# Tokens in another order on chip: keys of strides 2 to 8 side by side, the true order restored for the causal attention

## The chip, the core and the metric

The kernel runs on one core of a Trainium2 chip. The time is the device time of one execution, in microseconds. A core has a matrix engine (TensorE, rows PE, with its weight loads listed apart as PEld), a vector engine (DVE), a scalar engine (ACT), GpSimd (POOL) and the sync engine that issues the DMAs (SP). They work through their own lists of instructions and wait for each other by semaphores.

## The reference

The input is 16 sequences `q` of 512 tokens with 256 features, in fp32. Each goes through two layers: a coupling network of three cycles (A), a causal attention with rotary parts (B), the coupling network again (C), a small feature network (D), an attention with strided keys (E) with its own MLP, and the small network again (F). What matters here is that only B looks at the order of the tokens (rotary tables and causal mask), and that head `h` of E uses every `STRIDES[h]`-th key and value:

```python
STRIDES = [1, 1, 2, 2, 2, 2, 4, 4, 4, 4, 8, 8, 8, 8, 16, 16]
for h, stride in enumerate(STRIDES):
    k_s = k[:, h, ::stride, :]
    v_s = v[:, h, ::stride, :]
    scores = jnp.einsum('bqd,bkd->bqk', q[:, h], k_s) * scale
    attn = jax.nn.softmax(scores, axis=-1)
    outs.append(jnp.einsum('bqk,bkd->bqd', attn, v_s))
```

## The kernel before, in words

Everything of a sequence stays on chip from its load to its store. `X` holds the tokens on partitions (four tiles `t` of 128 tokens), `XT` the transposed normalized tokens: features on partitions, 512 tokens along the free dimension, two halves `f` of the features. Three sequences are on chip at a time. The table `TURN` (L30) is an order written out by hand: one pass over it works on three sequences in turn (A, B and C of newer ones, E and F of older ones), and every engine takes its own part of each step from it in this order. One pass is called a block below; there are 16 of them, some 215 us apart, and the 16 sequences overlap in them.

Token `t*128 + p` lies on partition `p` of tile `t` (L120), so in `XT` the tokens stand in their true order, column by column. Keys of stride `s` are then every `s`-th column. This touches four kinds of products of stage E on TensorE:

- `v.E`, the values (`values_part`, L619): the weights that are loaded are columns of `XT`, picked by `tile_of_keys` (L73). For heads of stride 1 to 4 a tile of 128 keys is every 4th column, for stride 8 and 16 every 8th and 16th. `V_PARTS` (L271) lists the pieces of tile 0: heads 0 to 9 with 128 keys, 10 to 13 with 64, 14 and 15 with 32; then tiles 1, 2 and 3. They stand in `TURN` as `part.E.0`, `part.E.1` and `v.E` (tiles 2 and 3).
- `content.E.g`, keys and queries of four heads (`content`, L582): the moving operand of the keys is `XT[:, c, f, 0:T:step]` with the first stride of the group, 1, 2, 4 or 8.
- `max.E.g`, a first product for the row maxima (`maxima`, L636): the second pair of heads in a group reads every second key of `HI`.
- `exp.E.g.r`, the scores that go to the exponential (`exponents`, L665): the loaded weights are columns of `MAT` by `tile_of_keys`; in group 0 (strides 1, 1, 2, 2) every 4th column, in group 1 every 2nd, in group 2 adjacent ones.

A fp32 product is two matmul instructions with a weight load each, so a call of `mm` on fp32 data shows as two rows of PE and two of PEld.

Around them, ACT copies the transposes from PSUM to `XT` (`copied`, L1066; the branch for B is L1076) and the attention's transposed result to `ATT` (`attended`, L1185; B is L1192). SP stores a finished sequence from `X` and loads the next one into the same place (L1366, L1368), after the wait for F's additions.

Of the kernel before, what the change touches and what calls it, by code (L numbers as in the profile page):

```python
# [14 lines left out]
P = 128  # L15
CH = 3
# [53 lines left out]
    return [[(t + u, (u * n[0], u * n[1]), n) for u in range(m)] for t in range(0, T // P, m)]  # L70


def tile_of_keys(columns, step, stride, t):  # L73


    if stride > 4:
        return columns[:, ::stride // step]
    return columns[:, (0, 2, 1, 3)[t] // step::4 // step]


def exp_rounds(s, g, T):
# [33 lines left out]
def build(nc, ins, out):  # L115
# [1 line left out]
    N, T, C = x_in.shape  # L117
    TT, KT = T // P, C // P
    assert T == 512 and C == 256
    x_v = x_in.rearrange("q (t p) d -> q p t d", p=P)  # L120
    o_v = out.rearrange("q (t p) d -> q p t d", p=P)
    _, e_tiles, _ = attention_shapes("E", T)
    E_SLOTS = sum(e_tiles)
    E_SLOT = [sum(min(n, t) for n in e_tiles) for t in range(TT)]
# [5 lines left out]
    with ctx:  # L130
# [109 lines left out]
        def steps_of(*names):  # L240
# [27 lines left out]
                                               for j in (2 * st[3], 2 * st[3] + 1) if j < 7])  # L268
        g_ready = Signal("g_ready", [st[1:3] for st in steps_of("relu") if st[3] == 3])
        dve_step, pool_step = sem("dve_step"), sem("pool_step")  # L270
        V_PARTS = [(0, 10, 4, 0), (10, 14, 8, 0), (14, 16, 16, 0)] + [  # L271
            (E_SLOT[t], E_SLOT[t] + sum(n > t for n in e_tiles), 1, t) for t in range(1, TT)]

        def tiles_of_groups(count):
# [41 lines left out]
        with nc.Block() as block:  # L316
# [73 lines left out]

            @block.sync
            def _(sp):
                sp.dma_start(X[:, 0], x_v[0]).then_inc(x_loaded[0], 16)
                for dst, src in first_loads:
                    sp.dma_start(dst, src, allow_slow_non_contiguous=True).then_inc(loaded_first, 16)

# [51 lines left out]
        with nc.Block() as block:  # L448

            @block.tensor  # L450
            def _(pe):
# [28 lines left out]
                def product(bank, key, pairs, rows=P, cols_=T):  # L480
                    dst = take(bank, *key)
                    for n, (lhsT, rhs) in enumerate(pairs):
                        last = mm(dst[0:rows, 0:cols_], lhsT, rhs, n == 0, n == len(pairs) - 1)
                    last.then_inc(full[bank], 1)

                def turned(b, key, src):
# [95 lines left out]
                def content(s, q, g):  # L582
                    c = q % CH
                    if s == "E":
                        in_xt("E", q)
                    else:
                        read_out(pe, "kvt", q)
                        read_out(pe, "ql", q)
                    if s == "B":
                        product(single_bank(), ("content", s, q, g, "q"), [(w_qdec[:, g, :], QL[:, q % 2, :])])  # L590
                        b = pair_bank()
                        dst = take(b, "content", s, q, g, "k", width=2)
                        for v in range(2):
                            half = slice(64 * v, 64 * v + 64)
                            last = mm(dst[:, v, 0:T // 2], w_kdec[half, g, :], KVT[half, q % 2, :])
                        last.then_inc(full[b], 1)
                        return
                    for w in "kq":
                        step = STRIDES[4 * g] if w == "k" else 1
                        product(single_bank(), ("content", s, q, g, w),  # L600
                                [(w_qk[:, f, "qk".index(w), g, :], XT[:, c, f, 0:T:step]) for f in range(KT)], cols_=T // step)

                def values(s, q):
                    c = q % CH
# [14 lines left out]
                def values_part(q, t):  # L619
                    c = q % CH  # L620
                    if t == 0:
                        in_xt("E", q)
                        dst = take(single_bank(), "v", "E", q, 0)
                    else:
                        dst = ps[:, J["v", "E", q, 0][0], :]
                    for first, end, stride, tile in V_PARTS:
                        if tile != t:
                            continue
                        h = first - E_SLOT[t]
                        for f in range(KT):  # L630
                            keys = tile_of_keys(XT[:, c, f, :], 1, stride, t)
                            last = mm(dst[0:min(P, T // stride), HD * first:HD * end], keys,
                                      w_v[:, f, HD * h:HD * (h + end - first)], f == 0, f == KT - 1)
                    return last

                def maxima(s, q, g, m):  # L636
                    keys, _, _ = attention_shapes(s, T)
                    if m == 0:
                        pe.wait_ge(hi_ready.sem, hi_ready.at(s, q, g, contents_in[s][-1]))
                    parts = parts_of((s, q, g), hi=True)  # L640
                    rounds = max_rounds(s, g, T)[m]
                    banks = [pair_bank(), pair_bank()]
                    dst = [take(banks[pair], "max", s, q, g, m, pair, width=2) for pair in (0, 1)]
                    for t, first, nk in rounds:
                        for a, b in parts:
                            for j in range(4):
                                at, step = first[j // 2], keys[4 * g] // keys[4 * g + j]
                                row = slice(ROWS * j, ROWS * j + ROWS)
                                last = mm(dst[j // 2][:, j % 2, at:at + nk[j // 2]], HI[row, a, t * P:(t + 1) * P],
                                          HI[row, b, 0:nk[j // 2] * step:step], (a, b) == parts[0],  # L650
                                          s == "E" and (a, b) == parts[-1])
                                if s == "E" and j % 2 and (t, (a, b)) == (rounds[-1][0], parts[-1]):
                                    last.then_inc(full[banks[j // 2]], 1)
                    if s == "B":
                        for pair in (0, 1):
                            for t, first, nk in rounds:
                                at = first[pair] + t * P
                                for b in range(4):
                                    for n in range(2):
                                        row = slice(ROWS * (2 * pair + n), ROWS * (2 * pair + n + 1))  # L660
                                        last = mm(dst[pair][ROWS * b:ROWS * b + ROWS, n, at:at + P], ident_b[row, row],
                                                  mask_q[row, b, :], False, True)
                            last.then_inc(full[banks[pair]], 1)

                def exponents(s, q, g, r):  # L665
# [4 lines left out]
                    for pair in (0, 1):  # L670
# [5 lines left out]
                        for kt, q0, at in exp_rounds(s, g, T)[r][1]:  # L676
                            for a, b in parts:
                                for n in range(2):
                                    j = 2 * pair + n
                                    row = slice(ROWS * j, ROWS * j + ROWS)  # L680
                                    if s == "B":
                                        columns = MAT[row, b, kt * P:(kt + 1) * P]
                                    else:
                                        columns = tile_of_keys(MAT[row, b, 0:T // STRIDES[4 * g]], STRIDES[4 * g],
                                                               STRIDES[4 * g + j], kt)
                                    last = mm(dst[0:m, n, at:at + T - q0], columns, MAT[row, a, q0:T],
                                              (a, b) == parts[0], (a, b) == parts[-1])
                        last.then_inc(full[bank], 1)
# [125 lines left out]
            def _(dve):  # L814
# [13 lines left out]
                def statistics(s, q):  # L828
                    c = q % CH
                    if s == "A":  # L830
                        dve.wait_ge(x_loaded[c], 16 * (q // CH + 1))
                    src = (XN if s == "E2" else X)[:, c]
                    for t in range(TT):
                        last = dve.bn_stats(stats[:, c, t, :], src[:, t, :])  # L834
# [230 lines left out]
            def _(act):  # L1065
                def copied(s, q):  # L1066
                    c = q % CH
                    for f in range(KT):
                        src = when_full(act, "xt", s, q, f)
                        if s in "AC":  # L1070
                            last = act.activation(XT[:, c, f, :], src, ACT.Copy, accum_out=means[:, c, f:f + 1])
                        elif s == "E2":
                            last = act.activation(XT[:, c, f, :], src, ACT.Identity, scale=c_gamma[:, f:f + 1],  # L1073
                                                  bias=c_beta[:, f:f + 1])
                        else:
                            last = act.activation(XT[:, c, f, :], src, ACT.Copy)  # L1076
                        freed(last, "xt", s, q, f)
# [107 lines left out]
                def attended(s, q):  # L1185
# [3 lines left out]
                    for f in range(KT):  # L1189
                        src = when_full(act, "att", s, q, f)  # L1190
                        if s == "B":
                            last = act.activation(ATT[:, f, :], src, ACT.Copy)  # L1192
                        else:
                            last = act.activation(ATT[:, f, :], src, ACT.Identity, bias=c_vb[:, f:f + 1])
                        freed(last, "att", s, q, f)
# [156 lines left out]

            @block.sync
            def _(sp):
                sp.dma_start(X[:, 1], x_v[1]).then_inc(x_loaded[1], 16)
                for dst, src in loads:
                    sp.dma_start(dst, src, allow_slow_non_contiguous=True).then_inc(loaded, 16)
                sp.wait_ge(zeroed, 4)
# [2 lines left out]
                for q in range(2, N):  # L1361
                    c = q % CH
                    if q >= CH:
                        for n in range(2):
                            read_out(sp, "mout", "F", q - CH, n)
                        sp.dma_start(o_v[q - CH], X[:, c]).then_inc(x_stored[c], 16)  # L1366
                        sp.wait_ge(x_stored[c], 16 * (q // CH))
                    sp.dma_start(X[:, c], x_v[q]).then_inc(x_loaded[c], 16)  # L1368
                for q in range(N - CH, N):
                    c = q % CH  # L1370
                    for n in range(2):
                        read_out(sp, "mout", "F", q, n)
                    sp.dma_start(o_v[q], X[:, c]).then_inc(x_stored[c], 16)
                for c in range(CH):
                    sp.wait_ge(x_stored[c], 16 * len(range(c, N, CH)))


# [35 lines left out]
```

## Time and profile before

| | |
|---|---|
| time, median of 3 runs | 3690.88 us (3689.16 to 3691.62) |
| span of the profiled execution, its first to its last instruction | 3688.1 us (its time with what lies around the span is not listed apart; the median of the runs stands 2.8 us above the span) |
| busy: PE, PEld, DVE, ACT, POOL | 94%, 54%, 62%, 51%, 26% |
| chain of work that ended last: PE, DVE, ACT | 82%, 12%, 3% |
| mean granted TensorE clock | 0.965 of 2.4 GHz |
| HBM traffic | 6 GB/s over the span |

Busy time is the share of the span in which an engine had an instruction under way; matmuls are pipelined, so their durations overlap, and what one costs is read from where the next begins. The granted clock is 1.00 (2.4 GHz) or 0.50 (1.2 GHz) at any moment, and a mean in between over a stretch.

### The profile page before, as it was taken

The numbers are of one execution on the slowest core, as the hardware profiler recorded it, in microseconds if no ns is written. First come the engines' busy times: TensorE is split into PE (matmuls) and PEld (weight loads), VectorE is DVE, ScalarE is ACT, GpSimd is POOL, SyncE is SP. The second block draws the span as 40 slices with busy tenths as digits, with TensorE's granted clock in tenths as the row PEclk, the third lists the DMA queues.
The fourth block names the chain that finished last, engine by engine and source line by source line (L and its number), as shares of the span: only waits on it lengthen the run. The fifth ranks groups of instructions, "written<-read, shape, count | busy, mean of one in ns | idle before, by whom it ended". The sixth has DMA issues, their size and how long they took to land.

```text
span 3688.1 us, 63212 instructions
## 1 busy us (share of the span) xinstructions
PE 3457.0 (94%) x24928; PEld 2002.6 (54%) x24928; DVE 2271.7 (62%) x4778; ACT 1887.2 (51%) x2919; POOL 955.1 (26%) x1069
## 2 busy tenths in 40 slices
PE   4789999999999999999999999999999999999876
PEld 3355556565555656555555655555565555555443
DVE  3446576666756666675666667566666756676442
ACT  2234655546465564646556464555646555564422
POOL 2213132331313232131222323122231313223111
PEclk8798999999999999999999999999999999999977
DMA  3000000000000000000000000000000000000000
GB/s 92 1 1 1 1 1 12 1 13 1 13 1 1 13 1 13 1 13 1 1 12 1 13 1 8 5 1 13 1 13 1 1 13 1 12 1 7 1 6 6
DMA packets 40882, 27.73 MB, mean 8 GB/s; under 512 B 19600, under 2 KB 39696, under 8 KB 40592
## 3 DMA queue, kind: packets, MB, share of 16 engines
q1 hardware_dynamic: 40592, 23.69, 2.2%
q8 instruction: 203, 3.33, 0.4%
q14 instruction: 87, 0.71, 0.1%
HBM read 15.30 MB, written 8.39 MB: 6 GB/s over the span
## 4 chain that ended last, share of the span: by engine, by line
PE 82%; DVE 12%; ACT 3%; issue 2%; POOL 0%; DVEq 0%; ACTq 0%; POOLq 0%
PE ps L478 74%; PE ps L489 8%; DVE MX L915 2%; DVE XN L843 1%; ACT other L1200 1%; DVE MX L909 1%; DVE XN L894 1%; DVE XN L891 1%; DVE XT L854 1%; DVE LT L881 1%; DVE XN L892 1%; DVE XT L853 1%; ACT PR L1174 0%; DVE stats L834 0%; DVE other L851 0%
## 5 line engine op out<-in xcount | busy, mean ns | idle before, releaser
L1174 ACT ACTIVATE PR<-ps 128x1024 f32<-128x1024 f32 (+3 forms) x592 | 524.5, 931 | 341.9 <-PE ps L478 340.6
L478 PE MATMUL ps<-MAT 32*128 32x512 f32 (+5 forms) x4928 | 593.3, 503 | 14.4 <-DVE MX L909 4.4
L915 DVE TENSOR_REDUCE MX<-ps 128x2 f32<-128x1024 f32 (+3 forms) x512 | 391.8, 818 | 203.7 <-PE ps L478 201.4
L1246 POOL TENSOR_TENSOR rstd<-var,neg_half 128x4 f32<-128x4 f32 x144 | 148.7, 1033 | 1311.3 <-DVE var L826 1183.5
L478 PEld LDWEIGHTS ps<-MAT 32*128 32x128 f32 (+2 forms) x4928 | 290.4, 199 | 262.4 <-issue 162.7
L478 PE MATMUL ps<-XT,cn_w 128*128 128x256 f32 x1536 | 367.6, 390 | 13.5 <-DVE XT L853 8.5
L478 PEld LDWEIGHTS ps<-XT,cn_w 128*128 128x128 f32 x1536 | 290.5, 193 | 99.7 <-issue 28.7
L478 PE MATMUL ps<-other,cn_w 128*128 128x512 f32 (+2 forms) x1152 | 321.0, 480 | 16.1 <-ACT other L1082 5.4
L921 DVE SCALAR_TENSOR_TENSOR MAT<-ps,MAT 128x512 f32<-128x512 f32 x128 | 88.5, 691 | 300.9 <-PE ps L489 300.3
L1281 POOL TENSOR_TENSOR MAT<-XN 128x512 f32<-128x512 f32 x128 | 167.3, 1307 | 402.4 <-DVE XN L894 241.8
L1304 POOL TENSOR_SCALAR_AFFINE_SELECT PR<-PR 128x512 f32<-128x512 f32 (+1 forms) x192 | 158.8, 827 | 410.0 <-ACT PR L1174 409.8
L909 DVE TENSOR_REDUCE MX<-ps 128x2 f32<-128x1024 f32 (+6 forms) x256 | 220.0, 902 | 59.6 <-PE ps L478 58.8
L1295 POOL CAST HI<-MAT 128x512 fp32r<-128x512 f32 (+3 forms) x256 | 146.4, 585 | 388.2 <-ACT MAT L1141 248.4
L478 PE MATMUL ps<-XT,w_up 128*128 128x512 f32 x512 | 245.7, 611 | 0.9 <-ACT XT L1073 0.9
L478 PE MATMUL ps<-HI 32*128 32x256 f32 (+4 forms) x3072 | 209.2, 360 | 36.4 <-DVE MX L915 25.4
L1082 ACT ACTIVATE other<-ps,cols 128x512 f32<-128x512 f32 x192 | 121.4, 683 | 228.3 <-PE ps L478 228.3
L478 PE MATMUL ps<-w_down,other 128*128 128x256 f32 x1024 | 227.4, 380 | 0.0
L843 DVE TENSOR_SCALAR XN<-X,mv,rstd 128x256 f32<-128x256 f32 x384 | 183.6, 540 | 67.6 <-POOL rstd L1246 67.0
L1200 ACT ACTIVATE other<-ps,cols 128x512 f32<-128x512 f32 x256 | 179.2, 795 | 71.4 <-PE ps L478 71.4
L478 PEld LDWEIGHTS ps<-HI 32*128 32x128 f32 x3072 | 117.3, 192 | 176.3 <-issue 136.5
L478 PEld LDWEIGHTS ps<-w_down,other 128*128 128x128 f32 x1024 | 193.4, 190 | 33.9 <-issue 7.7
L1183 ACT ACTIVATE AO<-ps 128x512 f32<-128x512 f32 x128 | 77.0, 602 | 255.5 <-PE ps L478 255.3
(158 smaller groups left out, 5718.2 us busy)
## 6 DMA issues: line engine op xcount, KB each, us to landing
X<-in_L_attn_x SPq DMA_DIRECT2D x16, 512.0 KB, 3.9
out<-X SPq DMA_DIRECT2D x16, 512.0 KB, 3.0
w_up<-in_L_attn_W SPq DMA_DIRECT2D x1, 1024.0 KB, 6.8
w_down<-in_L_attn_W SPq DMA_DIRECT2D x1, 1024.0 KB, 8.8
w_krope<-in_L_attn_W_krope SPq DMA_DIRECT2D x1, 512.0 KB, 4.4
w_qk<-in_L_attn_Wqkv SPq DMA_DIRECT2D x4, 128.0 KB, 4.4
cn_w<-in_L_ffn_cn_w SPq DMA_DIRECT2D x1, 256.0 KB, 4.2
w_qrope<-in_L_attn_W_qrope SPq DMA_DIRECT2D x1, 256.0 KB, 3.1
```

What stands on the lines that cost most here:

```text
L478: return pe.matmul(dst, lhsT, rhs, start=start, stop=stop, skip_group_check=True)
L489: last = pe.transpose(dst[:, t * P:(t + 1) * P], src(t), ident[:])
L843: last = dve.tensor_scalar(XN[:, c, t, :], src[:, t, :], mv[:, c, t, 0:1], rstd[:, c, t:t + 1], ALU.subtract, ALU.mult)
L909: last = dve.tensor_reduce(MX[:, t0:t0 + len(parts), at], src[:, :, 0:len(parts) * nk].rearrange("p j (t k) -> p t j k", k=nk), AX_X, ALU.max)
L915: last = dve.tensor_reduce(MX[:, t, at], src[:, :, a:a + nk[pair]], AX_X, ALU.max)
L1082: freed(act.activation(H1[:, area_of[s], m, :], src, ACT.Gelu, bias=c_b1[:, m:m + 1]), "h1", s, q, k, m)
L1174: freed(act.activation(PR[0:m, tile_of((s, q, g, r)), 2 * pair:2 * pair + 2, lo:T], ps[0:m, b:b + 2, 0:T - lo], ACT.Exp, scale=SCALE[s]), ...
L1200: last = act.activation(U[:, area_of[s], j, :], src, ACT.Relu, scale=c_mw1[:, j:j + 1], bias=c_mb1[:, j:j + 1])
L1246: pool.tensor_tensor(rstd[:, c, :], var[:, c, :], neg_half[:], ALU.pow).then_inc(rstd_ready.sem, 1)
L1281: pool.tensor_tensor(dst, a, b, ALU.add).then_inc(rope_sum.sem, 1)
L1295: pool.tensor_copy(HI[:, content_tile((s, q, g), w, hi=True), 0:n], MAT[:, content_tile((s, q, g), w), 0:n]).then_inc(hi_ready.sem, 1)
L1304: pool.affine_select(out=p, in_=p, compare_op=ALU.is_ge, fill=0.0, base=0, pattern=[[0, 4], [0, n], [1, P]], channel_multiplier=-1).then_i ...
```

## The change

The token of tile `t` on partition `64*d + m` is now `8*m + 4*d + t`. Tile 0 holds the tokens whose number is divisible by 4, its first half those divisible by 8; tiles 0 and 2 hold the even ones. Loads and stores of `X` are split in two halves of 64 partitions, each with 4 KB in one piece per partition where there were four pieces of 1 KB. In stage E the keys of strides 1 to 8 are adjacent columns; only stride 16 out of the keys of stride 8 still takes every second column. The keys of `content.E` come from whole tiles in the order 0, 2, 1, 3. The values of tile 0 for heads 10 to 13 go with those of heads 0 to 9 in one product of 128 keys and 224 columns, and the rows from 64 on are not read. For B, ACT's copy to `XT` writes the true order (inner step 8 elements, 32 bytes), and its copy to `ATT` goes back (inner step 128 elements, 512 bytes); both read PSUM in order. A, C, D and F don't depend on the order.

```diff
+def keys_in(columns, first_stride, stride, t=0, n=P):
+    if (first_stride, stride) == (8, 16):
+        return columns[:, 0:2 * n:2]
+    return columns[:, t * P:t * P + n]
+def tokens_of_keys(columns, stride):
+    if stride > 2:
+        return columns[:, 0:512 // stride]
+    tiles = columns.rearrange("p (v u n) -> p u v n", v=2, u=2)
+    return tiles[:, 0] if stride == 2 else tiles
+def first_token(t):
+    return (0, 2, 1, 3)[t]
...
-    x_v = x_in.rearrange("q (t p) d -> q p t d", p=P)
-    o_v = out.rearrange("q (t p) d -> q p t d", p=P)
+    x_v = x_in.rearrange("q (m d t) c -> q d m t c", d=2, t=TT)
+    o_v = out.rearrange("q (m d t) c -> q d m t c", d=2, t=TT)
...
-        V_PARTS = [(0, 10, 4, 0), (10, 14, 8, 0), (14, 16, 16, 0)] + [
+        V_PARTS = [(0, 14, 4, 0), (14, 16, 16, 0)] + [
...
-                sp.dma_start(X[:, 0], x_v[0]).then_inc(x_loaded[0], 16)
+                for d in range(2):
+                    sp.dma_start(X[64 * d:64 * d + 64, 0], x_v[0, d]).then_inc(x_loaded[0], 16)
...
                         step = STRIDES[4 * g] if w == "k" else 1
+                        tokens = [tokens_of_keys(XT[:, c, f, :], step) if w == "k" else XT[:, c, f, :] for f in range(KT)]
                         product(single_bank(), ("content", s, q, g, w),
-                                [(w_qk[:, f, "qk".index(w), g, :], XT[:, c, f, 0:T:step]) for f in range(KT)], cols_=T // step)
+                                [(w_qk[:, f, "qk".index(w), g, :], tokens[f]) for f in range(KT)], cols_=T // step)
...
-                            keys = tile_of_keys(XT[:, c, f, :], 1, stride, t)
-                            last = mm(dst[0:min(P, T // stride), HD * first:HD * end], keys,
+                            m = min(P, T // stride)
+                            keys = keys_in(XT[:, c, f, :], 8 if stride == 16 else 1, stride, first_token(t), m)
+                            last = mm(dst[0:m, HD * first:HD * end], keys,
...
-                                          HI[row, b, 0:nk[j // 2] * step:step], (a, b) == parts[0],
+                                          keys_in(HI[row, b, :], *strides, 0, n), (a, b) == parts[0],
...
-                                        columns = tile_of_keys(MAT[row, b, 0:T // STRIDES[4 * g]], STRIDES[4 * g],
-                                                               STRIDES[4 * g + j], kt)
+                                        columns = keys_in(MAT[row, b, :], STRIDES[4 * g], STRIDES[4 * g + j], kt, m)
...
+                        elif s == "B":
+                            last = act.activation(XT[:, c, f, :].rearrange("p (m d t) -> p t d m", d=2, t=TT),
+                                                  src.rearrange("p (t d m) -> p t d m", d=2, t=TT), ACT.Copy)
...
-                            last = act.activation(ATT[:, f, :], src, ACT.Copy)
+                            last = act.activation(ATT[:, f, :].rearrange("p (t d m) -> p m d t", d=2, t=TT),
+                                                  src.rearrange("p (m d t) -> p m d t", d=2, t=TT), ACT.Copy)
...
-                        sp.dma_start(o_v[q - CH], X[:, c]).then_inc(x_stored[c], 16)
-                        sp.wait_ge(x_stored[c], 16 * (q // CH))
-                    sp.dma_start(X[:, c], x_v[q]).then_inc(x_loaded[c], 16)
+                        for d in range(2):
+                            sp.dma_start(o_v[q - CH, d], X[64 * d:64 * d + 64, c]).then_inc(x_stored[c], 16)
+                        sp.wait_ge(x_stored[c], 32 * (q // CH))
+                    for d in range(2):
+                        sp.dma_start(X[64 * d:64 * d + 64, c], x_v[q, d]).then_inc(x_loaded[c], 16)
```

The order of the steps stays as it is. What changes in the lists is one pair of products per block on TensorE and the DMAs on SP. TensorE around the values of stage E, before (`ps` is PSUM, `w_v` the value weights, `x2` counts the calls):

```order
L478 MATMUL ps<-mask_q,ident_b 32x128 x16
L478 MATMUL ps<-w_v,XT 128x160 x2
L478 MATMUL ps<-w_v,XT 64x64 x2
L478 MATMUL ps<-w_v,XT 32x32 x2
L478 MATMUL ps<-PR,VB 17x384 x4
```

and with the change (L494 is the line that was L478):

```order
L494 MATMUL ps<-mask_q,ident_b 32x128 x16
L494 MATMUL ps<-w_v,XT 128x224 x2
L494 MATMUL ps<-w_v,XT 32x32 x2
L494 MATMUL ps<-PR,VB 17x384 x4
L494 MATMUL ps<-HI 128x128 x8
```

The two products of 64 keys went into those of 128. SP at the stores and loads of two blocks, before:

```order
L1366 DMA out<-X 128x4x256
L1368 DMA X<-in_L_attn_x 128x4x256
L1366 DMA out<-X 128x4x256
L1368 DMA X<-in_L_attn_x 128x4x256
L1366 DMA out<-X 128x4x256
```

and with the change:

```order
L1395 DMA out<-X 64x1024 x2
L1398 DMA X<-in_L_attn_x 64x1024 x2
L1395 DMA out<-X 64x1024 x2
L1398 DMA X<-in_L_attn_x 64x1024 x2
L1395 DMA out<-X 64x1024 x2
```

Each store and each load is now two DMAs of half the partitions.

## Rows read from the trace of the kernel before

**Rows 1.** The page: busy time of each engine, and the chain that ended last.

```profile
PE 3457.0 (94%) x24928; PEld 2002.6 (54%) x24928; DVE 2271.7 (62%) x4778; ACT 1887.2 (51%) x2919; POOL 955.1 (26%) x1069
...
PE 82%; DVE 12%; ACT 3%; issue 2%; POOL 0%; DVEq 0%; ACTq 0%; POOLq 0%
```

**Rows 2.** Timeline, weight loads of one block: start us, busy us, what, count.

```profile
1000.23 1.01 PEld L478 LDWEIGHTS ps<-w_v,XT 128*128 128x128 f32 x4
...
1001.38 0.56 PEld L478 LDWEIGHTS ps<-w_v,XT 128*64 128x64 f32 x4
...
1005.30 1.94 PEld L478 LDWEIGHTS ps<-w_v,XT 128*128 128x128 f32 x8
...
1082.70 1.86 PEld L478 LDWEIGHTS ps<-w_kv,XT 128*128 128x128 f32 x16 [0.24 <-issue]
```

**Rows 3.** Timeline, PE: keys and queries together, named by the keys' columns.

```profile
995.41 2.41 PE L478 MATMUL ps<-XT,w_qk 128*128 128x64 f32 x8
...
1014.01 2.88 PE L478 MATMUL ps<-XT,w_qk 128*128 128x128 f32 x8
...
1027.00 2.85 PE L478 MATMUL ps<-XT,w_qk 128*128 128x256 f32 x8
```

**Rows 4.** Timeline, PE: scores of group 1, then of group 0.

```profile
1074.39 1.15 PE L478 MATMUL ps<-MAT 32*128 32x512 f32 x8
...
1089.82 1.26 PE L478 MATMUL ps<-MAT 32*128 32x512 f32 x8
```

**Rows 5.** Waits: engine, line waited for, us in total, times, longest.

```profile
PE ps L570 <- DVE LT L881: 28.8, 16, 3.7
```

**Rows 6.** Stretches: length, busy (count) of PE, PEld, DVE, ACT, POOL, clock, DMA.

```profile
572.00:580.00 8.00, 7.78 (x118) 6.19 (x120) 4.99 (x11) 0.96 (x5) 3.25 (x4) 1.00 0.41 130
...
1007.00:1013.00 6.00, 6.00 (x50) 3.56 (x54) 3.58 (x12) 1.26 (x5) 1.09 (x2) 0.50 0.01 3
```

**Rows 7.** Timeline of SP: stores and a load of `X`, by issue.

```profile
785.79 0.38 SPq L1366 DMA_DIRECT2D out<-X  x1
788.73 0.37 SPq L1368 DMA_DIRECT2D X<-in_L_attn_x  x1
1000.54 0.38 SPq L1366 DMA_DIRECT2D out<-X  x1
...
1217.77 0.38 SPq L1366 DMA_DIRECT2D out<-X  x1
...
1433.61 0.38 SPq L1366 DMA_DIRECT2D out<-X  x1
```

**Rows 8.** Groups of ACT by form: busy us, mean ns, idle before.

```profile
L1174 ACT ACTIVATE PR<-ps 128x1024 f32<-128x1024 f32 x288 | 282.8, 1022 | 247.6 <-PE ps L478 247.2
...
L1076 ACT ACTIVATE XT<-ps 128x512 f32<-128x512 f32 x128 | 71.6, 600 | 101.4 <-PE ps L489 100.0
```

**Rows 9.** Timeline: both copies of B, and the product behind the second one.

```profile
1048.24 1.07 ACT L1192 ACTIVATE ATT<-ps 128x512 f32<-128x512 f32 x2
...
1051.68 3.72 PE L478 MATMUL ps<-w_o,ATT 128*128 128x256 f32 x16
...
1081.00 1.08 ACT L1076 ACTIVATE XT<-ps 128x512 f32<-128x512 f32 x2
```

**Rows 10.** DMA issues by line: count, KB each, median us to landing.

```profile
X<-in_L_attn_x SPq DMA_DIRECT2D x16, 512.0 KB, 3.9
out<-X SPq DMA_DIRECT2D x16, 512.0 KB, 3.0
...
w_qrope<-in_L_attn_W_qrope SPq DMA_DIRECT2D x1, 256.0 KB, 3.1
```

**Rows 11.** Timeline behind that load: statistics, normalization, transposes of A.

```profile
794.72 1.39 DVE L834 BATCH_NORM_STATS2 stats<-X 128x6 f32<-128x256 f32 x4
...
797.86 1.74 DVE L843 TENSOR_SCALAR XN<-X,mv,rstd 128x256 f32<-128x256 f32 x4 [1.13 <-POOL rstd L1246]
...
802.08 1.09 PE L489 MATMUL ps<-ident,XN 128*128 128x128 f32 x8
```

More of the change, by code:

```diff
@@ L70, in max_rounds @@
     return [[(t + u, (u * n[0], u * n[1]), n) for u in range(m)] for t in range(0, T // P, m)]
[L73 to L78, printed above, removed]
+def keys_in(columns, first_stride, stride, t=0, n=P):
[9 more added lines that the diff above has]
+    return (0, 2, 1, 3)[t]
 def exp_rounds(s, g, T):
@@ L482, in product @@
                     for n, (lhsT, rhs) in enumerate(pairs):
-                        last = mm(dst[0:rows, 0:cols_], lhsT, rhs, n == 0, n == len(pairs) - 1)
+                        to = dst[0:rows, 0:cols_]
+                        if len(rhs.shape) == 3:
+                            to = to.rearrange("p (v n) -> p v n", n=P)
+                        elif len(rhs.shape) == 4:
+                            to = to.rearrange("p (u v n) -> p u v n", u=2, n=P)
+                        last = mm(to, lhsT, rhs, n == 0, n == len(pairs) - 1)
                     last.then_inc(full[bank], 1)
@@ L646, in maxima @@
                             for j in range(4):
-                                at, step = first[j // 2], keys[4 * g] // keys[4 * g + j]
+                                at, n = first[j // 2], nk[j // 2]
                                 row = slice(ROWS * j, ROWS * j + ROWS)
-                                last = mm(dst[j // 2][:, j % 2, at:at + nk[j // 2]], HI[row, a, t * P:(t + 1) * P],
-                                          HI[row, b, 0:nk[j // 2] * step:step], (a, b) == parts[0],
+                                strides = (STRIDES[4 * g], STRIDES[4 * g + j]) if s == "E" else (1, 1)
+                                last = mm(dst[j // 2][:, j % 2, at:at + n], HI[row, a, t * P:(t + 1) * P],
+                                          keys_in(HI[row, b, :], *strides, 0, n), (a, b) == parts[0],
                                           s == "E" and (a, b) == parts[-1])
@@ L830, in statistics @@
                     if s == "A":
-                        dve.wait_ge(x_loaded[c], 16 * (q // CH + 1))
+                        dve.wait_ge(x_loaded[c], 32 * (q // CH + 1))
                     src = (XN if s == "E2" else X)[:, c]
@@ L1354, in _ @@
             def _(sp):
-                sp.dma_start(X[:, 1], x_v[1]).then_inc(x_loaded[1], 16)
+                for d in range(2):
+                    sp.dma_start(X[64 * d:64 * d + 64, 1], x_v[1, d]).then_inc(x_loaded[1], 16)
                 for dst, src in loads:
@@ L1365, in _ @@
                             read_out(sp, "mout", "F", q - CH, n)
-                        sp.dma_start(o_v[q - CH], X[:, c]).then_inc(x_stored[c], 16)
-                        sp.wait_ge(x_stored[c], 16 * (q // CH))
-                    sp.dma_start(X[:, c], x_v[q]).then_inc(x_loaded[c], 16)
+                        for d in range(2):
+                            sp.dma_start(o_v[q - CH, d], X[64 * d:64 * d + 64, c]).then_inc(x_stored[c], 16)
+                        sp.wait_ge(x_stored[c], 32 * (q // CH))
+                    for d in range(2):
+                        sp.dma_start(X[64 * d:64 * d + 64, c], x_v[q, d]).then_inc(x_loaded[c], 16)
                 for q in range(N - CH, N):
@@ L1372, in _ @@
                         read_out(sp, "mout", "F", q, n)
-                    sp.dma_start(o_v[q], X[:, c]).then_inc(x_stored[c], 16)
+                    for d in range(2):
+                        sp.dma_start(o_v[q, d], X[64 * d:64 * d + 64, c]).then_inc(x_stored[c], 16)
                 for c in range(CH):
-                    sp.wait_ge(x_stored[c], 16 * len(range(c, N, CH)))
+                    sp.wait_ge(x_stored[c], 32 * len(range(c, N, CH)))
 NAMES = ["L0_attn_x", "L0_attn_W_kv", "L0_attn_g_kv", "L0_attn_W_kdec", "L0_attn_W_vdec", "L0_attn_W_q",
```

## The prediction

> **What bounds the kernel now.** I read the page first: PE is busy 94% of the span and holds 82% of the chain that ended last, DVE 12%, ACT 3% [rows 1]. So time that TensorE saves is nearly all time that the kernel saves, and work added to ACT or SP counts only where it makes TensorE wait. Then the weight loads in a timeline, because the change alters how weights are read. The loads of the values, every 4th column of XT (16 bytes apart), take 1.94 us for 8, or 0.24 us each; the loads of adjacent columns of the same XT for the latent product take 1.86 us for 16, or 0.12 us each [rows 2]. The moving operand shows the same: keys and queries of a group together take 2.85 us with 256 key columns at stride 2, and 2.88 us, no less, with 128 key columns at stride 4; with 64 at stride 8 it is 2.41 us [rows 3]. The queries are the same four matmuls each time, so the step from 2 to 4 doubles what a column costs. Scores with weights at stride 4 take 1.26 us for 8 matmuls, at stride 2 only 1.15 [rows 4]. Stride 2 costs nothing that these rows show, stride 4 twice the time.
>
> **The change part by part, for one of 16 blocks.**
>
> *Values, tiles 1 to 3.* 12 loads (4 for tile 1, 8 for tiles 2 and 3) go from 0.24 to 0.12 us, and their matmuls of 96 and 32 columns are shorter than a load: 12 x 0.12 = 1.44 us.
>
> *Values, tile 0.* Now four loads of 128 keys take from 1000.23 to 1001.38, 1.15 us, and then four of 64 keys 0.56 us [rows 2]. The four of 64 go. The four of 128 get 224 columns instead of 160 and become bound by the stream: the group at 2.85 us streams 4 x 256 and 4 x 512 columns, 0.93 ns a column [rows 3], so 224 columns are 0.21 us and four are 0.84. Of the 1.15 us, 4 x 0.24 were loads and 0.2 the handover to the next shape, which stays: 0.84 + 0.2 = 1.04. Saved: 0.56 + 0.11 = 0.67 us.
>
> *Keys of group 2.* 128 adjacent columns are as short as a load, and so are 64 at stride 8. The group falls from 2.88 to about 2.41: 0.47, of which I take 0.45. Groups 0, 1 and 3 had no stride that costs: 0.
>
> *Scores of group 0.* Four rounds, each from 1.26 to 1.15: 0.44 us. The first round stands ahead of a product (L570) that waits for DVE's scaling of the latent in every block, 28.8 us over 16 [rows 5]; what is won ahead of it is waited for again. That leaves 0.33. Scores of groups 1 to 3 and the row maxima (second pair at stride 2, beside a first pair with twice its columns): 0.
>
> The sum is 1.44 + 0.67 + 0.45 + 0.33 = 2.89 us, and 16 blocks make 46. I take off 4 us for waits that come up at the edges, where few sequences overlap: **42 us**; bounds 35 (a quarter lost to waits) and 48 (the first round counted too).
>
> *The clock.* After the slow loads the granted clock falls to 1.2 GHz in many blocks: 1.00 over the values of the block at 571, but 0.50 from 1007 to 1013 [rows 6]. Nine of the 16 blocks have such a stretch right behind the values, four of 6.8 us and five of 3.4 us. Its price is read from the store that SP issues at the same place of every block: 214.75 us from 785.79 to 1000.54 without a low stretch, 217.23 us to the next with one of 6.8 us, 215.84 us to the next with one of 3.4 us [rows 7]. That is 2.5 and 1.1 us, and 4 x 2.5 + 5 x 1.1 = 15.5 us in all. The loads ahead of the fall now take half the time and the products behind them come sooner. I expect two thirds of the low stretches to go: **10 us**; bounds 0 and 16.
>
> *ACT's copies of B.* 32 copies to XT and 32 to ATT take 0.60 us each now [rows 8] and get inner steps of 32 and 512 bytes. No row shows ACT writing with a step. The near end is 0.60 us unchanged. The far end is the doubling per column that TensorE shows when it reads at 16 bytes [rows 2]: ACT takes 1.02 us for 1024 columns and 0.60 for 512 [rows 8], so 0.42 us goes with the columns and a copy becomes 1.02. That is the nearest row with such a step, so I take it. The pair to XT then ends at 1081.00 + 1.08 + 0.84 = 1082.92 instead of 1082.08 [rows 9], and the latent's loads, at 1082.70 now [rows 2], start some 0.25 us later: 16 x 0.25 = **4 us** lost. The pair to ATT ends at 1049.31 and its reader starts at 1051.68 [rows 9]; 0.84 us more is covered. Behind it on ACT wait the third layer of A and the exponentials of group 3, which come 0.8 us later; their readers on TensorE have other products ahead of them. If that cover is gone it costs up to 0.8 us a block, 13 in all. What speaks against the change here is the Trainium skill, "Advanced Engine Details and Errata", section SBUF Cachelines: an access that goes to another 16-byte line each time pays, and only two hits on a line absorb it. By that rule both copies are slow and the sum loses the 4 us; without it they stay at 0.60 us and it loses none. No row here shows it for writes.
>
> *SP.* Each store and each load becomes two DMAs. At the start and at the end one more issue of about 0.4 us [rows 7] lies open: **1 us**. In between, a load issued at 788.73 lands 3.9 us later [rows 10], at 792.6; DVE begins its statistics at 794.72 and ends the normalization at 799.60, and TensorE wants it at 802.08 [rows 11]. The slack is 2.1 + 2.5 = 4.6 us, less the 2.6 us by which the values and keys ahead of it get shorter: 2.0 us. Two more issues take 0.8. If the halves overlap, 256 KB lands in 3.1 us [rows 10] and nothing is late: 0. If they run one behind the other, the load takes 6.2 instead of 3.9 and the store 6.2 instead of 3.0, 5.5 more, and 4.3 us show in each of 13 blocks, 56 us. I take 0, because 512 KB in one piece lands in 3.9 us, and the bytes are the same. The Trainium skill, "SBUF — State Buffer", section "Can I just issue two DMAs to hit both halves?", says that two halves serialize, with 6% more rate than one. [...]
>
> **The sum** against the span of 3688.1 us: -42 - 10 + 4 + 1 = -47, so 3641 us. The median of the runs stands 2.8 us above that span: **3644 us**. A change under 0.2% (7.4 us) can't be told from none here.
>
> **The rivals.**
>
> 1. *The clock stays as it is.* The latent's product, too, has short matmuls, and the blocks get a new length and so meet the falls elsewhere. If nothing of the 15.5 us goes, the time is 3654. If all 16 blocks get 6.8 us (40 us instead of 15.5), it is 3679. For it: seven blocks have the same values and no fall, so the fall hangs on little. Against: the work right ahead of it is what the change speeds up. Chance 0.13.
> 2. *The loads of X come late*, by 1 to 4.3 us a block, 13 to 56 us: 3657 to 3700. For it: SP's store and load stand one behind the other. Against: the same bytes in fewer pieces. Chance 0.06, nearly all of it below 3680.
> 3. *Slower: ACT's strided copies become the bound.* Both pairs lie between a transpose and a product on TensorE. With an extra of D per copy the XT pair delays TensorE by 2D - 0.6 us, the ATT pair by 2D - 2.4, or by 2D - 1.5 through the exponentials. The gain without copies is 51 us, 3.2 a block; 4D - 2.1 = 3.2 gives D = 1.3. So it decides from copies of 1.9 us on, three times today's. At 2.4 us (D = 1.8) it costs 5.1 us a block, 82 in all: 3722. For it: an inner step of 512 bytes, farther than any row. Against: the doubling at 16 bytes did not grow at stride 8. Chance 0.05.
> 4. *The change doesn't do what it says*: the slow loads come from something else than the step, and stay slow: 3691. Against it: the same XT, the same 128 columns, half the time [rows 2]. Chance 0.03.
>
> **How the numbers follow.** The forecast has 0.70; its own range is 3628 (48 + 16 saved, 1 added) to 3667 (35 saved, no clock, 4 + 1 for ACT and SP, 6 more for ATT or loads). Better than 3624 has 0.03. With rival 1 whole but for its last third and the better part of rival 2, the range is **3624 to 3672**, and leaves out about 0.16. Faster by over 0.2%: 0.70 + 0.13 + 0.05 + 0.03 = 0.91. Slower: 0.05. Within 0.2%: 0.04.
>
> **What would show it.** The loads of the values at 0.12 us each and 320 of them, not 384. Keys and queries of group 2 at about 2.4 us, scores of group 0 at 1.15. The intervals between SP's stores at about 212 us, with fewer of 215.8 and 217.2. ACT's two copies at 1.02 us, or 0.60 if steps cost it nothing. No wait of DVE's statistics for a load. The prediction is wrong if the loads stay at 0.24 us, if PE shows idle time behind a copy of B, or if the low clock stays.

## The result, and the profile after

The changed kernel takes **3657.9 us** (median of 4 runs, 3652.58 to 3659.53) against 3690.65; ratio 0.9907, 95% interval 0.9893 to 0.9921. It is faster by 33 us, where 47 were forecast. The span of the profiled execution is 3657.6 us, 30.5 less than before.

The page after, busy times and the chain that ended last:

```profile
PE 3404.9 (93%) x24864; PEld 1942.6 (53%) x24864; DVE 2280.9 (62%) x4778; ACT 1912.0 (52%) x2919; POOL 957.0 (26%) x1069
...
PE 72%; DVE 19%; ACT 5%; issue 3%; POOL 0%; DVEq 0%; ACTq 0%; POOLq 0%
```

Against [rows 1] PE's share of the chain fell from 82 to 72%, and DVE's rose from 12 to 19%, ACT's from 3 to 5%. TensorE does its products in less time and now waits more.

Groups of weight loads by form, after (busy us, mean ns of one, idle before):

```profile
L494 PEld LDWEIGHTS ps<-w_v,XT 128*128 128x128 f32 x256 | 34.7, 191 | 2.5
...
L494 PEld LDWEIGHTS ps<-w_v,XT 128*32 128x32 f32 x64 | 3.2, 111 | 4.5 <-issue 4.5
```

There are 256 + 64 = 320 loads. A load's own duration overlaps that of the next, so what it costs is read from the spacing. The loads of tiles 2 and 3 in one block, and the timeline of TensorE in the same block, after, from the values to the keys of group 2 and then two pieces of the scores of group 0:

```profile
1221.77 0.97 PEld L494 LDWEIGHTS ps<-w_v,XT 128*128 128x128 f32 x8
```

```profile
1217.66 1.23 PE L494 MATMUL ps<-w_v,XT 128*128 128x224 f32 x7
...
1219.97 0.73 PE L494 MATMUL ps<-HI 32*128 32x128 f32 x16 [0.40 <-DVE MX L938]
1220.63 0.36 PE L494 MATMUL ps<-mask_q,ident_b 32*32 32x128 bf16 x32
1220.92 0.69 PE L494 MATMUL ps<-w_v,XT 128*128 128x96 f32 x4
1221.44 0.60 PE L510 MATMUL ps<-ident,AO 128*128 128x128 f32 x4
1221.88 0.98 PE L494 MATMUL ps<-w_v,XT 128*128 128x32 f32 x8
1223.03 0.66 PE L510 MATMUL ps<-ident,MX 128*128 128x128 f32 x4 [0.17 <-DVE MX L938]
...
1227.39 2.43 PE L494 MATMUL ps<-XT,w_qk 128*128 128x128 f32 x8
...
1303.82 1.14 PE L494 MATMUL ps<-MAT 32*128 32x512 f32 x8
...
1312.62 1.99 PE L494 MATMUL ps<-MAT 32*128 32x512 f32 x8
```

The eight loads of tiles 2 and 3 take 0.97 us, where [rows 2] had 1.94. Keys and queries of group 2 take 2.43 us instead of 2.88 [rows 3]; a round of scores of group 0 takes 1.14 instead of 1.26 [rows 4]. The third and fourth round follow each other as one row of eight products, which takes 1.99 us and before took 2.11. But behind the shorter values stand two waits for DVE's row maxima, 0.40 and 0.17 us of idle time.

The step of a block, by SP's stores at the same place as in [rows 7], after:

```profile
1004.42 1.28 SPq L1395 DMA_DIRECT2D out<-X  x2
...
1217.99 1.83 SPq L1395 DMA_DIRECT2D out<-X  x2
...
1431.54 1.13 SPq L1395 DMA_DIRECT2D out<-X  x2
```

A block takes 213.57 us, against 214.75 for a block before without a low clock. The clock in a stretch that answers to the second one of [rows 6], as long after the values of its block (columns as there):

```profile
1011.00:1017.00 6.00, 5.79 (x48) 3.06 (x40) 3.66 (x13) 3.48 (x5) 1.90 (x3) 1.00 0.11 26
```

It is at full clock, where it was 0.50. The first weight loads of the values in the first and in the 15th of the 16 blocks cut the span in three. Before:

```profile
353.06 1.01 PEld L478 LDWEIGHTS ps<-w_v,XT 128*128 128x128 f32 x4
...
3378.17 1.01 PEld L478 LDWEIGHTS ps<-w_v,XT 128*128 128x128 f32 x4
```

After:

```profile
363.25 0.68 PEld L494 LDWEIGHTS ps<-w_v,XT 128*128 128x128 f32 x4
...
3353.98 0.68 PEld L494 LDWEIGHTS ps<-w_v,XT 128*128 128x128 f32 x4
```

| us | before | after | difference |
|---|---|---|---|
| start, up to the first values | 353.1 | 363.3 | +10.2 |
| 14 blocks between | 3025.1 | 2990.7 | -34.4 |
| end, from the values of the 15th block | 309.9 | 303.6 | -6.3 |
| span | 3688.1 | 3657.6 | -30.5 |

Of the 34.4, 14 x (214.75 - 213.57) = 16.5 come from the work of the blocks. The other 17.9 are clock: low stretches in these 14 blocks fell from 11 with 51 us together to one of 3.4 us. The start, on the other hand, ran at the low clock for 123 us instead of 102.

Where a block gave time back shows in two more places. TensorE and ACT around the out projection, after:

```profile
1261.15 1.91 ACT L1218 ACTIVATE ATT<-ps 128x512 f32<-128x512 f32 x2
1262.87 0.43 ACT L1130 ACTIVATE other<-ps,cols 128x256 f32<-128x256 f32 x1
1263.32 1.28 ACT L1200 ACT_TABLE_LOAD   x1
...
1264.59 1.99 PE L494 MATMUL ps<-w_o,ATT 128*128 128x256 f32 x8
1264.61 1.92 ACT L1200 ACTIVATE PR<-ps 64x1024 f32<-64x1024 f32 x2
1266.43 0.81 ACT L1135 ACTIVATE other<-ps,cols 128x256 f32<-128x256 f32 x2
...
1266.94 1.99 PE L494 MATMUL ps<-w_o,ATT 128*128 128x256 f32 x8 [0.35 <-ACT other L1135]
```

The 16 products were one stretch of 3.72 us [rows 9]. Now the second eight wait for the PSUM bank that ACT's tanh (L1135) reads, and that tanh stands behind the longer copy to `ATT`, a table load and two exponentials. And at the copy to `XT`, after:

```profile
1294.52 2.01 ACT L1099 ACTIVATE XT<-ps 128x512 f32<-128x512 f32 x2
1294.85 1.50 PE L494 MATMUL ps<-other,cn_w 64*128 64x256 f32 x4
...
1295.66 0.29 PEld L494 LDWEIGHTS ps<-other,cn_w 64*128 64x128 f32 x2 [0.52 <-ACT XT L1099]
...
1296.71 2.00 PE L494 MATMUL ps<-w_kv,XT 128*128 128x64 f32 x16
```

A product of C (`tf.C.0`, four matmuls) waits halfway for a bank that the second copy of the transposes frees; it takes 1.50 us instead of the 1.02 of before:

```profile
1081.33 1.02 PE L478 MATMUL ps<-other,cn_w 64*128 64x256 f32 x4
```

The latent's product stands behind it and starts 0.18 us after the copies (1294.52 + 2.01 = 1296.53), without a wait for them. One block of each kernel (from 785 us before, from 1217 us after), matched instruction by instruction on TensorE, gives these steps: -3.12 us in values, keys and scores; +0.47 and +0.21 at DVE's row maxima; +0.12 at the latent's transposes, which wait for DVE's scaling; +0.62 at the out projection; +0.49 at `tf.C.0`. The sum, with small steps beside, is the 1.18 us.

### The profile page after: what moved, and what is told of

It is laid out like the page before. It is cut to its first block, busy times and chain, and to the rows that moved or that the text cites. A ratio compares the mean times of both kernels' runs of the same rounds, so it can differ in the third digit from the quotient of the medians.

```text
span 3657.6 us, 63116 instructions
## 1 busy us (share of the span) xinstructions
PE 3404.9 (93%) x24864; PEld 1942.6 (53%) x24864; DVE 2280.9 (62%) x4778; ACT 1912.0 (52%) x2919; POOL 957.0 (26%) x1069
## 4 chain that ended last, share of the span: by engine, by line
PE 72%; DVE 19%; ACT 5%; issue 3%; POOL 0%; DVEq 0%; ACTq 0%; POOLq 0%
PE ps L494 65%; PE ps L510 7%; DVE MX L938 4%; DVE G L977 3%; DVE XN L866 2%; DVE MX L932 2%; ACT PR L1200 1%; DVE XN L917 1%; DVE XN L914 1%; DVE XT L877 1%; ACT other L1227 1%; DVE LT L904 1%; DVE XN L915 1%; DVE XT L876 1%; ACT L1200 1%
## 5 line engine op out<-in xcount | busy, mean ns | idle before, releaser
L494 PE MATMUL ps<-MAT 32*128 32x512 f32 (+5 forms) x4928 | 574.9, 487 | 16.2 <-DVE MX L932 6.4
L494 PEld LDWEIGHTS ps<-MAT 32*128 32x128 f32 (+2 forms) x4928 | 274.3, 185 | 258.1 <-issue 151.3
L494 PE MATMUL ps<-XT,cn_w 128*128 128x256 f32 x1536 | 368.5, 391 | 13.5 <-DVE XT L876 8.5
L494 PE MATMUL ps<-other,cn_w 128*128 128x512 f32 (+2 forms) x1152 | 327.1, 480 | 18.5 <-ACT other L1130 5.9
L494 PEld LDWEIGHTS ps<-XT,cn_w 128*128 128x128 f32 x1536 | 291.1, 194 | 99.9 <-issue 28.5
L494 PE MATMUL ps<-XT,w_up 128*128 128x512 f32 x512 | 244.4, 608 | 0.9 <-ACT XT L1096 0.9
L494 PE MATMUL ps<-HI 32*128 32x256 f32 (+4 forms) x3072 | 206.3, 351 | 41.6 <-DVE MX L938 30.7
L494 PE MATMUL ps<-w_down,other 128*128 128x256 f32 x1024 | 227.4, 380 | 0.0
L494 PEld LDWEIGHTS ps<-HI 32*128 32x128 f32 x3072 | 115.3, 187 | 181.0 <-issue 125.3
L494 PEld LDWEIGHTS ps<-w_down,other 128*128 128x128 f32 x1024 | 193.4, 190 | 33.9 <-issue 7.7
```

Of the source, the lines that this page charges most:

```text
L494: return pe.matmul(dst, lhsT, rhs, start=start, stop=stop, skip_group_check=True)
```

## The experiments

Theory 1: the missing time went to ACT's two copies of B, which hold TensorE up at PSUM banks that ACT frees late. Theory 2: DVE sets the pace, so that what the copies give back is waited for again. Theory 3: the split loads and stores of `X` make DVE late. All ratios below are to the kernel before.

**1. Both copies in order.** The change, without restoring the order for B.

```diff
-  act.activation(XT[:, c, f, :].rearrange("p (m d t) -> p t d m", d=2, t=TT), src.rearrange(...), ACT.Copy)
+  act.activation(XT[:, c, f, :], src, ACT.Copy)
...
-  act.activation(ATT[:, f, :].rearrange("p (t d m) -> p m d t", d=2, t=TT), src.rearrange(...), ACT.Copy)
+  act.activation(ATT[:, f, :], src, ACT.Copy)
```

> The changed kernel, but ACT's two copies of B write in the order in which they read; the restoring of the true order is left out. Theory 1 (the missing gain went into ACT's doubled copies: in each block TensorE waits 0.49 us for the PSUM bank that the second XT copy frees, and 0.62 us at the out projection, whose second bank is freed behind the ATT copies in ACT's queue): both copies back at 0.60 us, blocks 1.1 us shorter, 16 x 1.1 = 18 us less than the changed kernel, about 3640. Theory 2 (TensorE has caught up with DVE's row maxima, which now set the pace): ACT's time only moves into those waits, 0 to 5 us less, about 3655. Theory 3 (the halved loads of X arrive late): the same as the changed kernel, 3658.

Measured: 3635.86 us (3634.99 to 3636.61), ratio 0.9847 (0.9831 to 0.9864); blocks of 212.44 us, copies of 595 and 593 ns. The copies cost 22 us, about what theory 1 said.

**2. Only the copy to ATT in order.** The second half of that edit.

> The changed kernel, but only ACT's copy to ATT writes in order (its part of the restoring is left out); the copy to XT keeps its step. Theory 1: the step of 0.62 us at the out projection goes, the one of 0.49 us at the tf product of C stays: 16 x 0.6 = 10 us less than the changed kernel, about 3648. Theory 2: 0 to 3 us less. Theory 3: the same, 3658.

Measured: 3648.06 us (3645.78 to 3650.51), ratio 0.9881 (0.9866 to 0.9895), blocks of 212.93 us. So the copy to `ATT` costs 0.64 us a block and that to `XT` the other 0.49: the two steps seen in the trace, each taken away with its copy.

**3. ACT reads with the step and writes in order.** The same permutation, with the two views exchanged; the reference is computed.

```diff
-  act.activation(XT[:, c, f, :].rearrange("p (m d t) -> p t d m", d=2, t=TT),
-                 src.rearrange("p (t d m) -> p t d m", d=2, t=TT), ACT.Copy)
+  act.activation(XT[:, c, f, :].rearrange("p (m d t) -> p m d t", d=2, t=TT),
+                 src.rearrange("p (t d m) -> p m d t", d=2, t=TT), ACT.Copy)
...
-  act.activation(ATT[:, f, :].rearrange("p (t d m) -> p m d t", d=2, t=TT),
-                 src.rearrange("p (m d t) -> p m d t", d=2, t=TT), ACT.Copy)
+  act.activation(ATT[:, f, :].rearrange("p (t d m) -> p t d m", d=2, t=TT),
+                 src.rearrange("p (m d t) -> p t d m", d=2, t=TT), ACT.Copy)
```

> The changed kernel with the same permutation, but ACT reads PSUM with a step and writes SBUF in order. If only writes with a step of 16 bytes or more double a copy: both copies at 0.60 us, and under theory 1 about 3640, under theory 2 about 3655. If reading PSUM with a step costs as much: both copies at 1.05 to 1.1 us and 3658. Under theory 3 3658 in any case.

Measured: **3636.45 us** (3634.15 to 3640.14), ratio 0.985 (0.9835 to 0.9865). ACT's groups by form in the changed kernel:

```profile
L1099 ACT ACTIVATE XT<-ps 128x512 f32<-128x512 f32 x32 | 32.2, 1109 | 14.6 <-PE ps L510 13.2
L1218 ACT ACTIVATE ATT<-ps 128x512 f32<-128x512 f32 x32 | 30.6, 1059 | 1.3 <-PE ps L510 1.3
```

and in this one:

```profile
L1099 ACT ACTIVATE XT<-ps 128x512 f32<-128x512 f32 x32 | 17.5, 595 | 14.8 <-PE ps L510 13.4
L1218 ACT ACTIVATE ATT<-ps 128x512 f32<-128x512 f32 x32 | 17.2, 593 | 1.3 <-PE ps L510 1.3
```

The rearrangement costs nothing that shows on the reading side. This is the best version found that computes the reference, 54 us below the kernel before and 21 below the change. Its out projection is one stretch again, and `tf.C.0` is back at 1.02 us; timeline of TensorE:

```profile
1039.11 3.72 PE L494 MATMUL ps<-w_o,ATT 128*128 128x256 f32 x16
...
1068.75 1.02 PE L494 MATMUL ps<-other,cn_w 64*128 64x256 f32 x4
```

**4. The loads as before.** `X` in one DMA over 128 partitions, so tokens stand in the old order and other keys than the reference's are used.

```diff
-  x_v = x_in.rearrange("q (m d t) c -> q d m t c", d=2, t=TT)
+  x_v = x_in.rearrange("q (t p) c -> q p t c", p=P)
...
-  for d in range(2):
-      sp.dma_start(X[64 * d:64 * d + 64, c], x_v[q, d]).then_inc(x_loaded[c], 16)
+  sp.dma_start(X[:, c], x_v[q]).then_inc(x_loaded[c], 16)
```

> The changed kernel with the loads and stores of X in one DMA of 128 partitions as before (so the tokens are in their old order and other keys are attended to). Theory 3: DVE's wait for the load of X (17 us in 13 blocks) goes, and 10 us or more with it, 3648 or less, and the first values start at about 353 us again instead of 363. Theories 1 and 2: blocks stay at 213.6 us; only the start wins some 0.8 us, 3656 to 3658.

Measured: 3657.21 us (3656.33 to 3657.4), ratio 0.9905 (0.989 to 0.992): no more than 0.7 us from the change, which is none. The wait that the split brought, in the changed kernel:

```profile
DVE stats L857 <- DMA X<-in_L_attn_x: 17.0, 13, 2.0
```

falls to 2.3 us here:

```profile
DVE stats L856 <- DMA X<-in_L_attn_x: 2.3, 3, 1.0
```

The time does not follow, and the first values start at 361.97 us, not at the 353 that theory 3 asked for. Theory 3 falls.

**5. Only the values' weights adjacent**, in the kernel before.

```diff
-  keys = tile_of_keys(XT[:, c, f, :], 1, stride, t)
+  keys = XT[:, c, f, t * P:t * P + min(P, T // stride)]
```

> The kernel before, in which only the value weights of stage E are adjacent columns (tile t of the keys is columns 128t onwards; so other keys than the reference's are used). Pieces of tile 0, keys of group 2, scores of group 0, both copies of ACT and the DMAs stay as before; copies stay at 0.60 us. Theory of the weight step: loads of the values fall from 0.233 to 0.112 us each; tile 1 gives 0.49 us a block and tiles 2 and 3 0.85, tile 0 perhaps 0.3; given back at the wait for DVE's row maxima 0.47 and at the transposes behind it 0.2; net about 1.0 us a block, 16 in all. The clock: if it is the slow weights of the values alone that the low stretches hang on, they go here too, some 15 us more, and the time is about 3658, with blocks of 213.5 to 214; if they hang on the keys, the scores or the copies as well, they stay and the time is about 3674. Rival (the weights' step is not what costs): 3691.

Measured: 3648.05 us (3646.14 to 3648.59), ratio 0.9882 (0.9867 to 0.9897). That is faster than either of the times that the text above gives for the weight step, and 10 us faster than the whole change: what the change does besides costs more here than it gains. The low clock goes with this edit alone: in the 14 blocks 3.4 us of it are left. Blocks take 213.20 us, so the values give 1.55 us, not the 1.0 expected; I had taken the unmerged pieces of tile 0 for slower than they are, and counted the waits in full. In the matched block the transposes of `MX` come 1.60 us earlier than before; in experiment 3, with tile 0 merged, they come 1.59 us earlier. The merge of `V_PARTS` shortens TensorE's work and moves no end here.

**6. Only the stepped copies**, in the kernel before: the same two `rearrange` writes, with tokens, loads and keys as they were; B's attention sees its tokens in another order.

> The kernel before, in which ACT's two copies of stage B write with the steps of the change, and nothing else is altered (so B's attention sees its tokens in another order than the reference's, and the output differs). Theory 1 (the doubled copies hold TensorE up, at the banks of PSUM): copies 1.06 to 1.11 us, blocks about 1.1 us longer, and with the start some 18 to 26 us more: 3709 to 3717. If the waits behind the copies can only show once the values are quick, because what stands between them is shorter then: under 8 us more, 3691 to 3699.

Measured: 3720.68 us (3706.09 to 3732.38, 5 runs), ratio 1.0085 (1.0058 to 1.0112). The five times go with their mean clock, from 0.967 at 3706 us to 0.957 at 3732. The median lies above the 3709 to 3717 expected, the profiled execution (3707.24 us) just below; what lowers the clock in the others was not traced. In the profiled one a block without a low clock, by SP's stores:

```profile
1225.84 0.38 SPq L1371 DMA_DIRECT2D out<-X  x1
1441.70 0.38 SPq L1371 DMA_DIRECT2D out<-X  x1
```

takes 215.86 us, 1.11 more than before, and the matched block shows it in the same two places, +0.61 and +0.49, at the same instructions:

```profile
1276.83 1.99 PE L478 MATMUL ps<-w_o,ATT 128*128 128x256 f32 x8 [0.34 <-ACT other L1113]
...
1304.76 1.51 PE L478 MATMUL ps<-other,cn_w 64*128 64x256 f32 x4
```

So the price of the copies in a block does not depend on the quicker values; theory 1 holds from this side too. Its start is only 3.5 us longer than before (first values at 356.61).

**7. Another order for TensorE**, on top of experiment 3.

```diff
-0:part.E.0 1:sum.B.2.1 1:max.B.3.2
-0:part.E.1 1:divide.B.1 0:v.E 1:shift.B.3
+0:part.E.0 1:sum.B.2.1 0:part.E.1
+1:max.B.3.2 1:divide.B.1 0:v.E 1:shift.B.3
```

> The kernel whose ACT reads PSUM with the step and writes in order (3636), with one step moved in the order of TensorE: the values of tile 1 (part.E.1, 0.44 us) stand ahead of the third round of B's first product of group 3 (max.B.3.2), which waits 0.4 us for DVE's row maxima in nearly every block. If that wait is a hole that other work can fill, a block loses 0.4 us and the time is about 3629 to 3631. If DVE's chain sets the pace there, or the hole opens again at the transposes of the row maxima (MX) behind it, the time stays at 3634 to 3638.

Measured: 3642.95 us (3641.48 to 3646.75), ratio 0.9871 (0.9856 to 0.9885): 6.5 us worse than experiment 3, and outside both of the expected ranges. TensorE in the same stretch, here:

```profile
784.50 0.69 PE L494 MATMUL ps<-w_v,XT 128*128 128x96 f32 x4
785.11 0.73 PE L494 MATMUL ps<-HI 32*128 32x128 f32 x16
...
786.55 0.98 PE L494 MATMUL ps<-w_v,XT 128*128 128x32 f32 x8
788.17 0.66 PE L510 MATMUL ps<-ident,MX 128*128 128x128 f32 x4 [0.64 <-DVE MX L938]
```

and in experiment 3:

```profile
782.06 0.73 PE L494 MATMUL ps<-HI 32*128 32x128 f32 x16 [0.40 <-DVE MX L938]
...
783.96 0.98 PE L494 MATMUL ps<-w_v,XT 128*128 128x32 f32 x8
785.11 0.66 PE L510 MATMUL ps<-ident,MX 128*128 128x128 f32 x4 [0.17 <-DVE MX L938]
```

The wait at `HI` is filled and opens again at `MX`, where 0.17 became 0.64. From the first load of the values (782.65 here, 779.75 there) to the transposes of `MX` it is 5.52 us instead of 5.36; the last round now comes to DVE 2.46 us behind that load, where it was 2.31. DVE's chain of row maxima sets the pace from `part.E.0` to `shift.B.3`. A block is 0.17 us longer, and the 14 blocks hold 10.2 us of low clock instead of 3.4; together they take 4.9 us more. The end takes 2.4 us more, for which no cause was sought. Theory 2 thus holds for this one stretch, and not for the copies.

## Why the prediction was right, and where it was off

The time lies in the range and the main mechanism is the predicted one. Step by step:

- **Loads, keys, scores.** Right, almost to the digit. Loads at 0.112 us, by their spacing, with 0.233 before; keys and queries 0.45 us less, as taken. Scores gain 0.12 us in three places, 0.36 and not the 0.44 that the prediction read as four rounds, since the third and fourth gain it once; the first is waited for again at the latent's transposes, as the prediction said. Gross, a block gained 3.12 us, or 3.00 with that first round taken off; the prediction had 2.89.
- **"I take off 4 us for waits that come up at the edges".** Mis-sized. The waits for DVE's row maxima are 0.47 + 0.21 us a block, 11 in all, and the one at the latent was counted apart. The values were to give 1.44 + 0.67 = 2.11 us and give 1.59, because of DVE. The row maxima stood in the profile of before as TensorE's second wait, 30.1 us in 28 times; the prediction did not ask what is due next behind each shortened piece. With the copies out of the way (experiment 3) a block comes to 212.43 us, 2.32 less than before: 37 us over 16 blocks, not 42.
- **ACT's copies: the duration.** Taken as 1.02 us, measured 1.11 and 1.06 (the rows under experiment 3). The doubling that TensorE showed at 16 bytes was the right row to go by, also for 512 bytes. Here the trace agrees with the Trainium skill, "Advanced Engine Details and Errata", section SBUF Cachelines, a penalty when each access goes to another line, for ACT's writes as well.
- **ACT's copies: their place and price, the step that failed.** The prediction put 4 us at the latent's loads and called the `ATT` pair "covered", with 13 us if that cover is gone. Measured: 1.13 us a block (213.57 - 212.44 in experiment 1), 16 us over the 14 blocks, and 7 to 8 us of the start, where experiments 1 and 3 have their first values at 356.1 and 355.1 us instead of 363.3. The `XT` pair costs 0.49, not 0.25, and one product ahead of the latent, at a PSUM bank. The `ATT` pair costs 0.62: the readers of its data are covered, as predicted, but the out projection needs a bank that a tanh further down ACT's queue has to free. The prediction followed those who read the copies' results, and not those who wait for the banks that ACT frees. Idle time of PE behind a copy of B was one of its own signs of being wrong, and it came.
- **The clock.** 10 us taken, bound 16, measured 17.9 in the 14 blocks; under-sized. The prediction counted the stretches right behind the values. Two blocks had another of 3.4 us some 85 us later, at 447.0 and 2611.0 us, and took 217.6 us each; these went too. Experiment 5 shows that quicker values are enough to take nearly all of it away. They don't rule it alone: in experiment 7, where the values are as quick, two stretches stand 7 to 8 us behind the start of the values, and in experiment 6, where they are slow, several blocks have none.
- **SP and the loads.** The 0 us for the loads is right, though DVE's statistics do wait, 17.0 us in 13 times, which the prediction named as a sign against it. Neither of its two cases came: halves of 256 KB land in 3.9 us (loads) and 3.2 us (stores), not 3.1, but the second is issued later, two issues taking 1.1 to 2.0 us, and a load in halves takes 4.8 us from its first issue to its last landing where one piece took 3.9, not 6.2. From the issue of a store to the landing of the load behind it, it is 8.7 us where it was 7.4 (medians of 13). These 1.3 us are less than the 2.0 us of slack that the prediction worked out, and no time is lost by them (experiment 4). The start, given 1 us with the end, lost 10.2.

By the terms of the sum: forecast -42 - 10 + 4 + 1 = -47. What the span shows is -16.5 (blocks) - 17.9 (clock) + 10.2 (start) - 6.3 (end) = -30.5. Had the copies been free, as in experiment 3, it would have been -54.7, below the forecast. In part it is luck that the time came out as near as it did: with the 10 us taken for the clock in place of 17.9 it would have been about 3666 us (an estimate), close to the upper end of the range, because the copies and the start cost more than the sum had. The end has two more blocks and 89 us at the low clock where it had 101; how its 6.3 us divide was not sought.

**Open:** why the start of the changed kernel spends 20 us more at the low clock. It isn't the loads: in experiment 4 the first values come at 362.0 us, with the same 123 us at the low clock. With the copy to `ATT` in order (experiment 2) they come at 359.0, with 116 us. Copies alone (experiment 6) and the rest without copies (experiment 3) each cost it 2 to 4 us, both together 10. A stretch of 3.4 us cost 1.1 us in a block [rows 7], so 20 us would be some 7 us (an estimate); by which way the copies and the quicker products together bring them on was not tried.

## What to carry to other kernels

When an engine's instruction gets longer, follow its queue to the next release of a PSUM bank and see who waits for that bank; the readers of the data are not the only ones that wait. If a copy has to rearrange, try the step on both of its sides: here the same permutation cost 21 us when written with a step, and nothing that shows when read with one. Before counting a shortened stretch in full, look for the instruction behind it that waits for another engine; that engine keeps its pace.

## What the runs showed of the hardware that was not expected

- ACT reads PSUM with an inner step as fast as in order: 595 ns for 512 columns at 512 bytes (the copy to `XT`) and 593 ns at 32 bytes (the copy to `ATT`), as in experiment 1. Writing SBUF takes 1109 ns at a step of 32 bytes (`XT`) and 1059 ns at 512 bytes (`ATT`). The Trainium skill, "Advanced Engine Details and Errata", section PSUM Cachelines, says that an access to PSUM that is not contiguous slows matmuls; for ACT's reads no run here shows any cost.
- A low clock can hang on a very small piece of work: the value weights of a block alone, 24 loads of 0.04 to 0.23 us each, made about half as long in experiment 5, took 48 of 51 us of it away in 14 blocks of the profiled execution.
